# Whole tiles stored at once, and the chosen patches of one place finished as a block of 128 rows

## The reference

```python
g = _gn(x)                                   # (x - mean) / sqrt(var + 1e-5) over each group
s = 0.5 * (|g[.., w+1] - g[.., w-1]| + |g[h+1, ..] - g[h-1, ..]|) + 0.5 * |g|     # zero padding
sp = s.reshape(n, 256, 8, 32, 8, 32).mean(axis=(3, 5))   # a score for each channel and 32 x 32 patch
mask = rank of sp among the 256 channels of that patch place < 128
out = x + g * mask                           # per patch: x * (1 + scale) + shift, or x unchanged
```

## Time and profile before

| | |
|---|---|
| median of three runs | 2007.05 us |
| profiled execution: span from first to last instruction | 2002.3 us |
| median less span | 4.8 us |
| busy share DVE / ACT / POOL / PE | 77 / 81 / 78 / 69% |
| DMA moved | 780.77 MB, 390 GB/s on average |

### The profile page before, as it was taken

One profiled execution on the slowest core, in us unless ns is written; L12 is line 12 of the kernel. 1 busy time (PEld: TensorE's weight loads), 2 busy tenths in 40 slices (PEclk: granted clock), 3 DMA queues, 4 the chain that ended last, 5 costly groups with the idle time before them and its releaser, 6 DMA issues.

```text
span 2002.3 us, 16132 instructions
## 1 busy us (share of the span) xinstructions
PE 1380.7 (69%) x3528; PEld 675.7 (34%) x3528; DVE 1542.1 (77%) x2087; ACT 1629.1 (81%) x2437; POOL 1555.6 (78%) x1113
## 2 busy tenths in 40 slices
PE   5989989868768867857787687768688876820000
PEld 2444444434333433423333333334333333410000
DVE  7878898789898869879898977888888977872110
ACT  4999999898879888888898879889789887851643
POOL 7899899768787777758877868758878786746776
PEclk9999999988889878879888788889788887965555
DMA  5899899999999999998999999999999999969997
GB/s 252 330 399 369 333 360 392 354 403 424 429 432 430 422 362 433 390 415 365 428 430 429 432 399 389 433 389 386 430 430 432 426 400 390 381 267 397 397 368 270
DMA packets 72082, 780.77 MB, mean 390 GB/s; under 512 B 21883, under 2 KB 21883, under 8 KB 35648
## 3 DMA queue, kind: packets, MB, share of 16 engines
q1 hardware_dynamic: 40896, 723.54, 87.3%
q0 software_dynamic: 31104, 56.45, 7.5%
HBM read 568.33 MB, written 329.25 MB: 448 GB/s over the span
## 4 chain that ended last, share of the span: by engine, by line
issue 20%; DMA 19%; DVE 17%; POOL 16%; ACT 15%; PE 9%; DVEq 3%; POOLq 1%; ACTq 0%; SPq 0%
DVE stats L911 8%; DMA again<-in_x_dram 8%; POOL pair L349 5%; DMA ring<-in_x_dram 4%; ACT again L803 4%; DMA out_dram<-again 4%; DVE sums L938 4%; PE vertical L707 4%; ACT thrown L872 4%; PE vertical L709 4%; POOL pair L355 3%; DVEq L902 3%; ACT vertical L866 3%; DMA ring<-in_x_dram,pair 2%; POOL scratch L349 2%
## 5 line engine op out<-in xcount | busy, mean ns | idle before, releaser
L707 PE MATMUL vertical<-ring,plus 128*128 128x512 f32 (+1 forms) x1200 | 664.4, 638 | 241.9 <-ACT vertical L866 240.9
L349 POOL TENSOR_TENSOR pair<-ring 128x960 f32<-128x960 f32 x360 | 638.3, 1793 | 26.0 <-DVE scratch L1082 17.9
L709 PE MATMUL vertical<-ring,minus 128*128 128x512 f32 (+1 forms) x1200 | 634.0, 612 | 0.0
L911 DVE BATCH_NORM_STATS2 stats<-ring 128x6 f32<-128x512 f32 x960 | 582.4, 680 | 40.4 <-DMA ring<-in_x_dram 31.9
L872 ACT ACTIVATE thrown<-ring,record 128x1024 bf16<-128x1024 f32 x480 | 548.2, 1142 | 8.8
L938 DVE TENSOR_REDUCE sums<-pair 128x2 f32<-128x1920 f32 (+1 forms) x212 | 455.0, 2146 | 126.8 <-POOL pair L349 126.2
L803 ACT ACTIVATE again<-again,coef 128x1024 f32<-128x1024 f32 x324 | 374.4, 1227 | 107.2 <-DMA again<-in_x_dram 106.9
L707 PEld LDWEIGHTS vertical<-ring,plus 128*128 128x128 f32 x1200 | 240.9, 211 | 514.6 <-ACT vertical L866 292.4
L355 POOL TENSOR_TENSOR pair<-ring 128x960 f32<-128x960 f32 x120 | 270.5, 2254 | 141.8 <-DVE sums L938 116.3
L709 PEld LDWEIGHTS vertical<-ring,minus 128*128 128x128 f32 x1200 | 250.0, 208 | 295.5 <-issue 295.5
L349 POOL TENSOR_TENSOR scratch<-ring 128x960 f32<-128x960 f32 x120 | 215.3, 1794 | 152.8 <-ACT kept L822 103.3
(11 more groups left out here) (118 smaller groups left out, 1443.2 us busy)
## 6 DMA issues: line engine op xcount, KB each, us to landing
ring<-in_x_dram SPq DMA_DIRECT2D x59, 4096.0 KB, 20.4
again<-in_x_dram SPq DMA_DIRECT2D x89, 2048.0 KB, 16.6
out_dram<-again SPq DMA_DIRECT2D x89, 2048.0 KB, 16.3
out_dram<-in_x_dram SPq DMA_DIRECT2D x29, 2048.0 KB, 28.6
kept<-in_x_dram SPq DMA_DIRECT2D x4, 4096.0 KB, 22.7
out_dram<-kept SPq DMA_DIRECT2D x8, 2048.0 KB, 13.8
ring<-in_x_dram SPq DMA_DIRECT2D x4, 1024.0 KB, 7.8
out_dram<-ring SPq DMA_DIRECT2D x2, 2048.0 KB, 9.7
```

The lines of the kernel that those rows point to most:

```text
L349: return nc.gpsimd.tensor_tensor(part.rearrange("p (r c) -> p r c", r=PATCH), xs[:, w, :, 2:], xs[:, w, :, 0:PATCH - 2], ALU.subtract)
L707: nc.tensor.matmul(v[:, first:end], plus[:], xs[:, first + 2 * PATCH:end + 2 * PATCH], start=True, stop=False)
L709: done = nc.tensor.matmul(v[:, first:end], minus[:], xs[:, first:end], start=False, stop=True)
L911: nc.vector.bn_stats(stats[:, k, :], buffer[:, k * BN:(k + 1) * BN])
```

## The change

**Buffers.** The three ring buffers, `kept` and the three half-tile slots become four ring buffers (any tile) and three sets of four patch columns, `slots`. No engine program has a loop any more: all 64 tiles are written out.

**Dense and unchanged.** A tile is stored as it is, as soon as it is loaded (`store_tile`), with three groups of exceptions: the last tile of images 0 to 2 and the last four of image 3 wait in the ring for the ranking and are finished whole (7 tiles); the first six of image 3 are copied in DRAM during image 0 (12 half tiles instead of 29). 51 tiles are stored at once.

**Blocks.** For each place (band and column) of an image the 128 chosen channels are one index column: 128 rows of 4 KB at 256 KB times the channel. `max_index` in every ranking round gives the channels, TensorE turns the list into columns (`turn_order`), and VectorE makes row numbers and, from the group of each channel, factor and offset for each row (`factors_of`, four parts of 16 places). Rows in a dense tile get a number beyond the end and are skipped. A block is four places. During tile t of the next image, GpSimd scatters block t-2 and gathers block t, and ScalarE finishes block t-1 (`o0` to `o3`). The blocks of image 3 come after everything, alternately gathered and scattered.

**Horizontal sums.** |a - b| = 2 max(a, b) - a - b. VectorE makes the sum of maxima of each patch with one SCALAR_TENSOR_TENSOR with accumulation, GpSimd adds the first two and last two columns (`end_columns`), and the sum over all comes from the statistics (`means`). Only the tile beside the ranking (first of images 1 to 3) still goes by differences on GpSimd and absolute sums on ScalarE. Vertically: five patches TensorE and ScalarE as before, three GpSimd and ScalarE.

```diff
-RING = 3
-SLOTS = 3
+RING = 4
+DENSE_FROM = (LAST, LAST, LAST, TILES - RING)
+COPIES = (2, 1, 1, 1, 1, 1, 1, 1, 1, 1, 1, 0, 0, 0, 0, 0)
+BLOCK = 4
+SETS = 3
+ORDER = "p0 a0 v0 a1 p1 a2 o0 v1 a3 a4 o1 p2 v2 a5 o2 a6 v3 o3 a7 v4".split()
...
+            def gather_block(n):                                   # GpSimd
+                image, first = n // BLOCKS, n % BLOCKS * BLOCK
+                pool.wait_ge(rows_ready, image + 1)
+                if n >= SETS:
+                    pool.wait_ge(scattered[n % SETS], 16 * BLOCK * blocks_before(n))
+                for j in range(BLOCK):
+                    row = rows[image % 2][:, first + j:first + j + 1]
+                    nc.gpsimd.indirect_dma_start(slot(n, j), None, x_rows, ...)
...
+            for tile in range(ALL_TILES):
+                if n >= 2:
+                    scatter_block(n - 2)
+                wait_loaded(pool, tile)
...
+                    if n >= 0:
+                        gather_block(n)
+                    difference(tile, 0)
+                    end_columns(tile)
+                    difference(tile, 1)
+                    columns_at_edge(tile)
+                    difference(tile, 2)
...
+            for n in range(STREAMED, ALL_BLOCKS):
+                gather_block(n)
+                if n >= STREAMED + 1:
+                    scatter_block(n - 1)
...
+            def load_tile(tile):                                   # SyncE
+                b = tile % RING
+                if tile >= RING:
+                    before = tile - RING
+                    sp.wait_ge(place_ready, placed_until(before + 1))
+                    sp.wait_ge(edges_free, before + 1)
+                    wait_summed(sp, before)
+                    sp.wait_ge(stored[b], 16 * stores_until(before))
+                sp.dma_start(ring[b][:], x[tile]).then_inc(loaded[b], 16)
...
+            def inner_across(tile, patches):                       # VectorE
+                xs = by_patch(ring[tile % RING])
+                if across(tile):
+                    settle()
+                for w in patches:
+                    if across(tile):
+                        nc.vector.scalar_tensor_tensor(out=larger[w % 2][:].rearrange("p (r c) -> p r c", r=PATCH),
+                                                       in0=xs[:, w, :, 2:], scalar=0.0, in1=xs[:, w, :, 0:PATCH - 2],
+                                                       op0=ALU.add, op1=ALU.max, accum_out=maxima[:, w:w + 1])
...
+            def step(tile):
+                statistics(tile + 1, 0)
+                statistics(tile + 1, 1)
+                inner_across(tile, (0, 1))
+                if tile % TILES:
+                    keep_statistics(tile - 1)
+                    keep_sums(tile - 1)
+                inner_across(tile, (2, 3))
+                statistics(tile + 1, 2)
+                inner_across(tile, (4, 5))
+                end_columns(tile)
+                statistics(tile + 1, 3)
+                rows_at_edge(tile)
+                inner_across(tile, (6, 7))
+                minus_mean(tile + 1)
+                columns_at_edge(tile)
+                finish_across(tile)
...
                     nc.vector.max(largest[:], left)
                     settle()
+                    nc.vector.max_index(picked[:, 8 * k:8 * k + 8], largest[:], left)
                     nc.vector.match_replace(out=left, in_to_replace=largest[:], in_values=left, imm_value=-1.0)
...
+            def factors_of(image, part):
+                q = slice(part * PART, (part + 1) * PART)
+                settle()
+                if image:
+                    dve.wait_ge(finished, BLOCKS * (image - 1) + (part + 1) * PART // BLOCK)
+                nc.vector.tensor_tensor(one_hot, group_bank[:, q]..., group_numbers[:]..., ALU.is_equal)
+                for kind, made in enumerate((factor, offset)):
+                    settle()
+                    nc.vector.tensor_tensor(weighted..., one_hot..., table_bank[:, :, kind, :]..., ALU.mult)
+                    settle()
+                    done = nc.vector.tensor_reduce(made[:, q], weighted, AX.X, ALU.add)
```

More of the change, by code:

```diff
@@ L30 @@
 PATCHES = BANDS * COLS
-RING = 3
-SLOTS = 3
-LOOPED = (TILES - 1) // RING
+ALL_TILES = IMAGES * TILES
 LAST = TILES - 1
+RING = 4
 BN = 512
 CHUNKS = PIX // BN
[L43 to L48, removed]
@@ L78 @@
[L78 to L85, removed]
@@ L88 @@
[L88 to L91, removed]
-OUT, OUT_RANKING = (0, 2, 2, 2, 1, 2, 2, 1, 2, 2, 1, 2, 2, 2, 2, 0), 2
-assert sum(OUT) + OUT_RANKING == HALVES and HALVES % SLOTS == 0
-ORDER_FIRST = "A0 S0 d a0 B0 v0 a1 a2 v1 v2 a3 a4 a5 a6 v3 a7 v4".split()
@@ new lines, with ranked_beside, placed, placed_until @@
+ORDER_RANKING = ("p0 v0 a0 p1 a1 p2 a2 p3 a3 p4 a4 p5 a5 v1 p6 a6 p7 a7 p8 v2 p9 o0 p10 o1 v3 o2 o3 v4"
+                 .split())
+def ranked_beside(tile):
+    return tile % TILES == 0 and tile > 0
+def placed(tile):
+    down = [(DOWN, w) for w in range(PE_DOWN, COLS)]
+    return [*down, *((ACROSS, w) for w in range(COLS))] if ranked_beside(tile) else down
+def placed_until(tile):
+    return sum(len(placed(t)) for t in range(tile))
+def across(tile):
+    return 0 if ranked_beside(tile) else COLS
@@ new lines, in scatter_block @@
+            def scatter_block(n):
+                image, first = n // BLOCKS, n % BLOCKS * BLOCK
+                if n % BLOCKS == 0:
+                    for b in range(RING):
+                        sent = [t for t in range(b, TILES * (image + 1), RING) if not (t // TILES == image and dense(t))]
+                        pool.wait_ge(stored[b], 16 * stores_until(sent[-1]))
+                    if image == IMAGES - 1:
+                        pool.wait_ge(copied, 16 * sum(COPIES))
+                pool.wait_ge(finished, n + 1)
+                for j in range(BLOCK):
+                    row = rows[image % 2][:, first + j:first + j + 1]
+                    nc.gpsimd.indirect_dma_start(out_rows, bass.IndirectOffsetOnAxis(ap=row, axis=0),
+                                                 slot(n, j), None, bounds_check=ROWS - 1,
+                                                 oob_is_err=False).then_inc(scattered[n % SETS], 16)
@@ L534, in _ @@
[L534 to L545 removed]
+                nc.gpsimd.tensor_scalar(factors[:, 0, :], scale[:], 1.0, 1.0, ALU.mult, ALU.add)
@@ new lines, in _, with copy_half @@
+            copies = [(TILES * (IMAGES - 1) + h // 2, h % 2) for h in range(sum(COPIES))]
+            def copy_half():
+                tile, h = copies.pop(0)
+                pixels = slice(h * HALF, (h + 1) * HALF)
+                sp.dma_start(out[tile, :, pixels], x[tile, :, pixels]).then_inc(copied, 16)
+            for quarter, signal in enumerate(first_loaded):
+                part = slice(quarter * PIX // 4, (quarter + 1) * PIX // 4)
+                sp.dma_start(ring[0][:, part], x[0, :, part]).then_inc(signal, 16)
@@ L676, in _, with mean @@
+            for tile in range(TILES * (IMAGES - 1) + DENSE_FROM[-1], ALL_TILES):
+                store_finished(tile)
+            for b in range(RING):
+                sp.wait_ge(stored[b], 16 * stores_until(ALL_TILES - RING + b))
+            for s in range(SETS):
+                sp.wait_ge(scattered[s], 16 * BLOCK * len(range(s, ALL_BLOCKS, SETS)))
+            sp.wait_ge(copied, 16 * sum(COPIES))
         @block.tensor
         def _(pe):
-            def mean(tile, r):
+            def mean(tile):
```

1131 lines of the change are left out of this document (417 added, 714 removed).

## The result

The changed kernel takes 2413.2 us, the median of four runs (2410.54 to 2417.53), against 2006.89 us for the kernel before, run beside it. The ratio is 1.2018 (1.1999 to 1.2038). The forecast of 2,055 us had the sign, but the time lies 358 us above it and outside the range.

The account below looks back on a forecast made before the run. It took DMA to bound the kernel, engines at 85% behind. Image 0 459, images 1 and 2 972, image 3 439 and tail 180 sum to 2,050 us; with 4.8 more, 2,055 us, range 1,945 to 2,180.

Parts of the forecast that it names:

- The other engines stay below: In the analysis of tiles: ScalarE needs 393 us an image and GpSimd 20 us a tile, so neither sets the pace.
- What bounds the kernel before: Whole span of the old kernel: DMA sets the pace, 94.8% of 2,002 us, with engines at 85% behind it.
- DMA work: Traffic of the whole run: 776 MB against 780.8, 1,894 us against 1,898, so nothing is taken away.
- rival 3: Indirect rows come slower or too late; 2,189 us at three quarters of the rate; chance 0.15.
- DMA 393 is below: Image 0 with its ranking: 393 us of DMA work lies under the 459 us forecast from VectorE.
- The cover of gathers: Block gathers are wanted one tile and 7 us after issue; costed at nothing, with lost cover left to rival 3.
- P = 25.1: VectorE's us for a tile: 22.55 of work plus 2.6 waiting on GpSimd at the shared port; break-even 23.55.
- The ranking: After an image's analysis: 40 us in which VectorE does nothing else, against 32 us before.
- The tail: Blocks of image 3 at the end: 180 us, with GpSimd issues at 1.29 us each; DMA 167 just below.
- Rival 1: Maxima slip between GpSimd's differences and DMA stays the only bound: 1,950 us, faster; chance 0.30.
- P = 22.6: VectorE's us for a tile under Rival 1, giving 419 us for image 0 and 1,950 us in all.
- Rival 2: Accumulation halves the rate of VectorE's maxima, each taking 1.0 us more: 2,450 us; chance 0.07.

Follow-up runs that it names:

- 4 KB kernel: Changed kernel with the three edits, and each plain load and store of a tile cut into eight DMAs with 4 KB packets; 2121.08 us, ratio 1.0556.
- three edits: Changed kernel: GpSimd makes differences before scatter and gather, VectorE combines sums before freeing border columns, last tile gathers after the ranking's GpSimd work; 2319.64 us.
- the last run: 4 KB kernel with GpSimd's vertical differences replaced by a memset of the same size, their sums left out; 2069.94 us, ratio 1.0308.

## Why the prediction was wrong

The step that failed is "The other engines stay below". It summed ScalarE (393 us an image) and GpSimd (20 us a tile) as if each could use its idle time when it liked. Both sums held (362 us for 393; 316.5 us for 16 tiles of GpSimd, 320 forecast). What it left out was that the new scatter stands at the head of GpSimd's list, waits for the last finish of ScalarE, and has behind it the difference that ScalarE needs first. The prediction never says what is queued behind the waiting scatter. Opened on either engine's side, the ring is worth 69 or 95 us by itself; the rest lay behind it, in the late rows.

Step by step, with the 4 KB kernel (forecast 2,050 of span, 2121.0 measured) for what remains once the ring and the late rows are mended:

| | forecast | after | three edits, 4 KB | without vertical differences too |
|---|---|---|---|---|
| image 0 | 459 | 490 | 475.5 | 458 |
| image 1 | 486 | 594 | 476.3 | 474 |
| image 2 | 486 | 564 | 483.7 | 484 |
| image 3 | 439 | 551 | 472.1 | 439 |
| tail | 180 | 217 | 213.4 | 214 |

- **What bounds the kernel before** (the DMA, engines at 85% behind it): nothing speaks against it. It was no guide to a kernel with other queues.
- **DMA work**: bytes right. In the 4 KB kernel images 1 and 2 are DMA-bound at 476 and 484 against the 474 worked out and 486 forecast, and stay at 474 and 484 when the maxima are relieved. In the changed kernel rows cost 25.8% of 2416.4 us for 239.17 MB, 2.61 us a MB against the 2.55 taken from the earlier trace rows, and by the same measure the kernel before has 2.66 (7.5% of 2002.3 for 56.45 MB); the slowdown at large pitch that rival 3 feared doesn't show. The split by stage was wrong: loads and stores run ahead of the analysis, so 180 MB and not 155 had moved by the first ranking, and "DMA 393 is below" is 458 in the last run.
- **The cover of gathers** ("wanted one tile and 7 us after it"): named as cover, and priced only at 3 us a tile. When the ring was opened, rows came up to 39.5 us late, 514.9 us over the run. This is the half of rival 3 that was real; at first the ring hid it.
- **P = 25.1**: low. The own work was right: 1.16 us a maximum, 0.08 for its accumulator. The wait for the port was put at 2.6 us a tile; in image 0 it was nearer 5 (tiles of 27.4 to 27.5 us), and the kernel without blocks has (468 - 62.7) / 15 = 27.0. The average of a busy GpSimd was the wrong model. After a tile the edges are freed, GpSimd starts at once, and just then VectorE reaches its next two-input instructions, so they meet every time. This is the excess of 16 us in image 0 and 33 in image 3 of the 4 KB kernel. The agreement of the last column with the forecast, 458 for 459 and 439 for 439, is luck: there the port costs the maxima nothing, and waits for loads (40.3 us in image 0, 27.1 in image 3) and for the ranking stand in its place.
- **The ranking**: its 40 us fit image 0 (418 of VectorE's work and 40 of waits are the 458 of the last column). Before the three later rankings GpSimd's `drain` behind scatters and gathers added stalls of 39.7, 12.6 and 3.3 us, which the prediction didn't have.
- **The tail**: issues come every 1.3 us, as forecast, when they come. But GpSimd stands for 22.1 us ahead of its third block of scatters in the tail, for a finish that waits for its gather, and for 7.3 us at the next gather. At that time, 2219 to 2259, the DMA share is 1.02 and 1.01, and the dense stores, issued from 2217.8 us on, go out beside the gathers. So it was 217 and not 180. That the dense stores are the cause isn't tested, and smaller packets don't mend it: it stays at 212 to 217 in each version here that does the blocks.
- **Rival 1** (maxima slip between differences, 1,950): false. Even with no blocks at all images 1 and 2 take 468 and 467 us against 466 and 465 for everything before. And with the maxima at 1163 ns, the P = 22.6 of this rival, the time is 2069.94 and not 1,950: the DMA holds image 0 at 458, not 419.
- **Rival 2** (the accumulation halves the maxima, 2,450): its time is within 1.5% of the 2413.2 measured, and it is false. 488 maxima have a mean of 1371 ns, 1163 with the port free, and not 2.1 us; alone one takes 1.16 us, as the two-input L925 without accumulation took 1.17. The Trainium skill's rule for this instruction with two SBUF sources other than bf16, "Vector Engine (DVE) Microarchitecture Reference", § Points that are easy to get wrong, doesn't hold for these 960-element maxima; the measurement decides. Who reads only the total would take the wrong story.

No version run here makes the change a gain; the best that computes everything loses 4.6%. With eight maxima a tile and the vertical differences on GpSimd, the analysis without its second pass is already later at the last ranking (1884 us) than the kernel before with it (1793). Of the 406 us lost, 292 come back with the three edits and 4 KB packets, and 51 more when the vertical differences are left out. In the last column, against the stages of the earlier trace rows, image 0 is still 56 us longer than before (458 to 402), images 1 and 2 are 8 and 19 longer, image 3 is 21 shorter and the tail 5 longer: 67 us of span.

## What to carry to other kernels

Busy sums say what an engine can do, its list says when. For each new wait write down what is queued behind it on its engine, who needs that, and whether that is what the wait itself waits for; here the answer was a ring of 33.7 us a tile that no sum shows. When small indirect transfers and large plain ones run together, compare their packet sizes before their bytes. And a total that fits a rival proves nothing until the rival's own row has been read; nor does a stage that fits the forecast, as 458 for 459 did here by another limit.

## What the hardware showed that I had not expected

- Two queues on the same DMA engines got nearly equal numbers of packets through, whatever their size: about 10 rows of 4 KB a us beside 12 packets of 32 KB, about 50 beside as many of 4 KB, about 100 alone. In the kernel with the three edits, 4 KB packets for the plain traffic gave 199 us, although the plain queue's packets then took 63.4% of 2121.0 us for the same bytes, 1,345 us, against 54.9% of 2416.4, 1,327.
- A GpSimd `drain` that followed four indirect scatters and four gathers stood for 39.74 us, with the DMA engines at 1.02 in a window of 20 us inside it. With the scatters alone ahead of it, it stood for 32.56, and with nothing indirect ahead it didn't wait.
- The port between VectorE and GpSimd stops even small instructions until the other engine's is done: an 8-element one with two inputs went from 0.17 to 2.10 us, and a maximum from 1.16 to 3.07.
- A SCALAR_TENSOR_TENSOR of 960 float32 elements with accumulation takes 1.16 us, and reading its accumulator 81 ns more.
